# Six bfloat16 products of a tile of ones per group in two stages of a graph network, on TensorE

## What is computed

```python
# layer 0: two SAGE convolutions, mean over incoming edges, 128 -> 150 -> 128
neigh = segment_sum(h[src], dst) * deg_inv
h     = h @ W_self + neigh @ W_neigh + b        # twice, relu between
x     = layernorm(x + h)
# layer 1: messages along edges
ef  = (relu(edge_attr @ We1 + be1) @ We2 + be2) * sigmoid(ts * Wt + bt)
msg = relu(concat(x[src], ef) @ Wn1 + bn1) @ Wn2 + bn2
x   = layernorm(x + segment_sum(msg, dst) + x)
```

## Time and profile before

| | |
|---|---|
| median of 3 runs | 10547.17 us (10542.76 to 10547.24) |
| the profiled execution | 10652.36 us |
| its span, first to last instruction | 10648.5 us |
| PE, PEld busy | 6164.5 us (58%), 4857.4 us (46%) |
| POOL busy | 6516.8 us (61%) |
| DVE, ACT busy | 3810.3 us (36%), 2663.4 us (25%) |
| mean granted TensorE clock | 0.725 of full speed |
| group products begin to end, stage two | 3119 to 5858 us, 375 groups |
| group work begins to ends, stage three | 5888 to 10637 us, 625 groups |

### The profile page before, as it was taken

One profiled execution on the slowest core, in us unless ns is written; L12 is line 12 of the kernel. 1 busy time (PEld: TensorE's weight loads), 2 busy tenths in 40 slices (PEclk: granted clock), 3 DMA queues, 4 the chain that ended last, 5 costly groups with the idle time before them and its releaser, 6 DMA issues. The chain is left out here.

```text
span 10648.5 us, 114426 instructions
## 1 busy us (share of the span) xinstructions
PE 6164.5 (58%) x31767; PEld 4857.4 (46%) x31767; DVE 3810.3 (36%) x9118; ACT 2663.4 (25%) x3928; POOL 6516.8 (61%) x6882
## 2 busy tenths in 40 slices
PE   3456566666643334444444567666766667676676
PEld 2344444444433333343333455545555555555555
DVE  6766666666520111111111223233333333333333
ACT  3433333333200000000000233333333333333333
POOL 5555556566646666666665566666666666666665
PEclk9855666777756666666665788888888878888888
DMA  2334444555524444444432333333333333333332
GB/s 71 88 98 124 125 141 152 156 163 179 175 93 144 158 135 148 150 152 148 152 102 56 112 109 109 110 110 110 111 111 110 112 111 113 112 113 119 107 122 91
DMA packets 568848, 1305.10 MB, mean 123 GB/s; under 512 B 161231, under 2 KB 374499, under 8 KB 547476
## 3 DMA queue, kind: packets, MB, share of 16 engines
q1 hardware_dynamic: 348209, 846.63, 23.4%
q0 software_dynamic: 220000, 451.00, 15.7%
HBM read 1190.99 MB, written 106.10 MB: 122 GB/s over the span
## 5 line engine op out<-in xcount | busy, mean ns | idle before, releaser
L1465 POOL DMA_INDIRECT messages_rows<-y_d,src_idx x3125 | 2948.0, 943 | 1825.8 <-issue 955.4
L954 POOL DMA_INDIRECT sum_x_rows<-in_x,sum_x_edges x1875 | 1792.3, 956 | 1238.3 <-issue 532.5
L954 POOL DMA_INDIRECT sum_z_rows<-z_d,sum_z_edges x1875 | 1775.2, 947 | 1022.3 <-issue 536.0
L1509 PE MATMUL messages_p_msg<-Wm_e,messages_gated 128*128 128x128 f32 x6250 | 1102.5, 337 | 1046.1 <-DVE messages_gated L1573 941.0
L1509 PEld LDWEIGHTS messages_p_msg<-Wm_e,messages_gated 128*128 128x128 f32 x6250 | 961.7, 238 | 1373.6 <-DVE messages_gated L1573 1068.5
L1040 PE MATMUL sum_z_win<-sum_z_hot,sum_z_rows 128*128 128x64 f32 x3750 | 829.9, 330 | 1073.6 <-DVE sum_z_sums L1170 636.9
L1040 PEld LDWEIGHTS sum_z_win<-sum_z_hot,sum_z_rows 128*128 128x128 f32 x3750 | 894.7, 276 | 1153.3 <-DVE sum_z_sums L1170 677.2
L1568 DVE TENSOR_TENSOR messages_rows<-messages_p_msg,messages_rows 128x640 f32<-128x640 f32 x625 | 515.0, 824 | 2046.0 <-remote 1367.1
L1121 ACT CAST sum_x_counts<-sum_x_build 128x294 f32 (+3 forms) x1250 | 778.3, 623 | 1838.3 <-DVE sum_x_build L1236 1154.4
L1523 PEld LDWEIGHTS messages_win<-messages_hot,messages_rows 128*128 128x128 f32 x6250 | 864.6, 208 | 488.9 <-issue 431.8
L1051 PE MATMUL sum_x_build<-sum_x_key_hot,sum_x_low_hot 128*128 128x294 bf16 (+3 forms) x1250 | 508.3, 407 | 940.3 <-ACT sum_x_counts L1121 547.3
(11 more groups left out here) (175 smaller groups left out, 6820.3 us busy)
## 6 DMA issues: line engine op xcount, KB each, us to landing
messages_when<-in_edge_weight SPq DMA_DIRECT2D x125, 1600.0 KB
sum_x_split<-x_parts_d SPq DMA_DIRECT2D x238, 675.5 KB
sum_z_split<-z_parts_d SPq DMA_DIRECT2D x238, 672.0 KB
messages_attr<-in_edge_attr SPq DMA_DIRECT2D x125, 800.0 KB
counts_d<-sum_x_counts SPq DMA_DIRECT2D x17, 3136.0 KB
sum_z_counts<-counts_d SPq DMA_DIRECT2D x17, 3136.0 KB
messages_rows<-y_d,src_idx POOLq DMA_INDIRECT x3125
sum_x_rows<-in_x,sum_x_edges POOLq DMA_INDIRECT x1875
```

Of the source, the lines that this page charges most:

```text
L954: nc.gpsimd.indirect_dma_start(out=rows[:, s % depth, j, :], out_offset=None, in_=table, in_offset=bass.IndirectOffsetOnAxis(ap=edges[:, b ...
L1465: nc.gpsimd.indirect_dma_start(out=rows[:, g % DEPTH, j, :], out_offset=None, in_=d["y"], in_offset=bass.IndirectOffsetOnAxis(ap=t.src_idx ...
L1509: last = nc.tensor.matmul(msg[:, j * P:(j + 1) * P], gated[:, g % GATEDS, j * P:(j + 1) * P], t.Wm_e[:], start=True, stop=True)
```

## The change

A constant and two insertions. In `window_tile`, in stage two alone (`not counting`), six products of the tile of ones with itself, repeated to 512 columns, go into the bank `win[g % 2]`, behind the waits for `sums_added` and `hot_ready` and ahead of the wait for `rows_arrived`. In stage three six such products go into the two banks of `p_edge` by turns, behind the wait for `gated_ready` and ahead of that for `msg_added`. Nothing reads their results: each bank's next real product has `start=True` and overwrites the columns that are used.

```diff
+WARM = 6
@@ window_tile
                     pe.wait_ge(hot_ready, g + 1)
                     if counting:
                         pe.wait_ge(hot_summed, g + 1)
+                    if not counting:
+                        for _ in range(WARM):
+                            nc.tensor.matmul(win[g % 2][:], t.ones16[:], t.ones16[:].unsqueeze(1).to_broadcast([P, 4, P]), start=True, stop=True)
                     pe.wait_ge(rows_arrived[g % depth], (g // depth + 1) * 16 * TILES)
@@ sum_messages, tensor
                 for g in groups(s, 2):
                     pe.wait_ge(gated_ready, g + 1)
+                    for i in range(WARM):
+                        nc.tensor.matmul(p_edge[:, i % 2, :], t.ones16[:], t.ones16[:].unsqueeze(1).to_broadcast([P, 4, P]), start=True, stop=True)
                     wait_for(pe, msg_added, g)
```

## The result

The changed kernel took 10871.67 us (median of 4 runs, 10867.65 to 10872.27), the kernel before 10545.72 us beside it (4 runs, 10542.76 to 10547.24): ratio 1.0309, 95% interval 1.0291 to 1.0326, 326 us more. Slower was forecast, at 11080 us: 533 us over the median, rounded down from a sum of +564 us.

The account below looks back on a forecast made before the run. It took POOL's gathers as the floor, with POOL's waits for PE and late PE results above it. Stage three +474 and stage two +90 gave +564 us on 10547, 11111, rounded to 11080 us; range 10100 to 11750 us.

Parts of the forecast that it names:

- The sum: Whole kernel: stage three +474 us and stage two +90 us, +564 us together; forecast rounded down to 11080 us.
- One of the six: Each added 512-column product: 0.22 us at full clock, 0.44 at half; six take 1.3 and 2.6 us.
- Stage three, the share on the path: Six per group total 1000 us in stage three; 0.68 of it, as for message products, is path: +680 us.
- the 680 us: Stage three: the added products' time on the path, before 206 us gained by the clock.
- The clock: Stage three: mean clock rises from 0.81 to 0.93, gaining 206 us on PE's 1597 us of chain.
- Stage two: Six per group total 790 us, mostly covered by POOL's gathers; 15%, 120 us, less some 30 for clock: +90 us.
- A: Rival: higher clock after stage three's pauses wins, faster, about 10150 us, or 9260 if POOL's waits go; chance 0.33.
- B: Rival: all hidden, late results come whatever PE does, in both stages; 10547 us, give or take 20; chance 0.12.
- C: Rival: more lateness, six come in full, 1790 us, 12340 us at most; 0.17 of forecast's chance above 11440.
- D: Rival: products of ones don't count for the clock, which stays 0.81 and 0.61; +800 us, 11350 us; chance 0.1.
- Two signs named beforehand: Group times: stage three up from 7.6 to about 8.3 us, stage two to about 7.6 us.
- The others: Signs: clock above 0.85 in stage three, 0.65 in stage two; message products beginning 1.3 to 2.6 us behind DVE's gating.

Follow-up runs that it names:

- the later pair beside 10650 us: Six products of 512 columns per group in stage three alone, added to the kernel before, timed beside it at 10650.25 us: 10837.29 us, ratio 1.0173.

## Why the prediction was right, and where its terms were off

The sign and the stage were right, and so was the way: the six stand behind the wait, PE's pauses stay, and POOL's waits for PE lengthen. The sum was not: 564 us for 326. And the sign holds for surroundings like those of its rows alone: on two other chips the same change costs nothing (0.9995), and the prediction names no such condition. That its rows and the timing were both of the slow ones was luck.

*One of the six* was put at 1.3 us for six at full clock and 2.6 at half. From their start to that of the next products it is 1.30 us at full clock and 2.53 at half; the records show 1.47 and 2.74, and exposed they cost 1.20 us. This was right. At the stage's real mix they were 1175.5 us busy in stage three, for 1000 forecast.

*Stage three, the share on the path.* This is the term that failed: 0.68, taken from the message products as their neighbour. The four groups of products that were there before came down from 3460 to 3105 us busy, 355 us, and the six added 1175.5, so PE had 820 us more to do and stage three took 298 us more, 0.36 of it. In the later pair beside 10650 us it is less still: the six 1158.3 us, the four groups 3070 us, so 768 us more, for 182 us, 0.24. The prediction said itself that some of the 680 us would take the place of late results, and took 31 us off for it; the chain shows some 580 us that the six displaced. In this loop, which waits for something else in part, the neighbour's share of the chain was some twice too much for the insertion.

*The clock.* 0.93 was forecast, 0.86 granted. Behind a long pause the clock is at half as before (0.50 from 8014 to 8017), and the pauses stayed. The saving by it was forecast at 206 us; by the same formula with 0.86 it would be 1597 x (1 - 0.81/0.86) = 93 us. The records of the four groups lost 355 us, on the path or off it, and how much of that is on it no run shows. The largest part, 142 us, is the second products', which went from 956.3 to 814.2 us. The Trainium skill's rule, in "TensorE: Matmul & The Clock Gate" (section "Why this matters for your kernels"), that idle gaps between bursts are what costs throughput, agrees with this: the trace still has 1043.7 us of gaps ahead of L1512.

*Stage two* was put at +90 us and came to +36. The cover, POOL's gathers, held. The share on the path was about twice too much: +90 of 790 us is 11%, and the stage grew by 36 us, 5% of the 736.6 us that the six are busy there, and by 160 us with twenty-four, 8% of their 2081.5.

*The rivals.* A is excluded: no run is faster for the products beyond its interval, and where PE alone is the bound the six cost 1.20 us a group. B, all hidden, is false in the timing forecast and true wherever before takes 9057 us, for another reason than the one given: not because late results come when they come, but because POOL's gathers are the bound. C, that longer stretches at full clock bring more lateness and the six come in full, did not come: 326 us of 1790, and DVE's late results are 205 in both kernels. Twelve products do cost more than in proportion to six on the faster chips, but because the cover ends. D is excluded by the clocks. Two signs named beforehand came short: stage two's group time went from 7.2 to 7.3 us and not to 7.6; stage three's went to 7.9 and not to 8.3. The others came: 0.86 and 0.72 for a clock above 0.85 and 0.65, and message products 2.6 us behind the end of DVE's gating at 8014.91.

## What to carry to other kernels

Before filler work is priced by its share of the chain, find the engine whose floor lies above the filled one and how far: here six products fit under 6.24 us of gathers and twelve did not. Filler behind the wait that makes the pause lengthens the loop and leaves the pause; a higher granted clock was no gain where the engine with the higher clock was not the bound. And time a change where it is to run: the same two kernels stood at 1.0309 and at 0.9995.

## What the runs showed of the hardware that was not expected

The same kernel before took 9057 and 9058 us on two chips, and 10548, 10650 and 10644 us in three jobs on a third. In the slower surroundings results of PE reach DVE several us behind the end of its records (5.8, 6.5 and 4.0 us in the three looked at), at full clock. In the kernel after 198 of 205 come while POOL stands still, in the kernel before 89 of 205. In the faster surroundings no wait of these in stage three is put down as "remote", and the one looked at ended 0.11 us behind the products. With three fifths of the gathers gone the slower chip shows 0.11 us too, and stage three needs 4.35 us a group against 4.20 us on the faster chip (the former with the narrow six). With all five gathers it needs 7.5 against 6.24. What carries the results so late, and why one chip does it and two don't, no run here tells. A version with the products ahead of PE's wait for gated rows, in the pause itself (16 products of 192 columns in the window bank's unused ones), was written but has no time: DVE reads that bank meanwhile, and nothing orders the two. So whether filling the pause would pay is untested.
